# A four-stage attention program on one core: the self-attention values of a decoder kept 64 wide, and a new timetable

## The chip, the cores and the metric

One core of one Trainium2 chip runs the whole program. The time is the device time of one launch in microseconds; lower is better. Everything is fp32.

## The reference, cut to what matters

Four attention stages follow each other on two batches of 512 tokens, 128 wide, with a context of 77 rows, 64 wide. Stages L0, L1 and L3 are short. Stage L2 is a decoder of 6 layers, 16 heads of width 64:

```python
def _mha(s, t, kv_w, q_w, o_w, o_b, mask):
    k, v = jnp.split(s @ kv_w, 2, axis=-1)
    k, v, q = (_heads(k), _heads(v), _heads(t @ q_w))
    scores = jnp.einsum('bhqd,bhkd->bhqk', q, k) * D ** (-0.5)
    scores = jnp.where(mask[:, None] == 0, jnp.float32(-1000000000.0), scores)
    attn = jax.nn.softmax(scores, axis=-1)
    o = jnp.einsum('bhqk,bhkd->bhqd', attn, v)
    return o.transpose(0, 2, 1, 3).reshape(...) @ o_w + o_b

def step(t, p):                                   # one layer, 6 of them
    tn = _ln(t, norm_g, norm_b); t = _mha(tn, tn, skv, sq, sow, sob, tgt_mask) + t
    tn = _ln(t, norm_g, norm_b); t = _mha(src, tn, ckv, cq, cow, cob, src_mask) + t
    tn = _ln(t, pg, pb);         t = t + (jax.nn.relu(tn @ w1 + b1) @ w2 + b2)
```

The mask inputs leave at most the last 128 of the 512 tokens as keys of the self attention (the first 384 or more have a 0 in the mask, and what is 0 is masked out), so the kernel has a path, the unit `FAST`, in which a self-attention head has 128 keys. A flag computed on the chip chooses between it and a general path (`WIDE`), which the inputs here don't take.

## The kernel before, in words

The work of a layer is in four phases: self attention of batch 0 and of batch 1 (s0, s1), cross attention of batch 0 and of batch 1 (x0, x1). A phase is a list of chunks, each 128 query tokens by a group of heads: in self attention 4 groups of 4 heads, 4 chunks each. A group of four heads is two pairs of heads; a pair is 128 of the 1024 head columns.

For each chunk TensorE makes the scores of all heads of the group (`scores`, line 969: one matmul, 512 columns for self attention), VectorE adds the mask by a minimum and takes the row minimum (line 1363), ScalarE takes the exponentials one head at a time (line 1156), VectorE takes reciprocals of the sums (line 1371), GpSimd multiplies (line 642), TensorE transposes the weights block by block (`turn`, line 979), and ScalarE or VectorE copies them to the tile `PT` (lines 1166 and 1380), which has two places, one for each of two groups in flight. When all four chunks of a group are there, TensorE multiplies by the values (`attend`, line 999). All groups of a phase accumulate in one PSUM bank, `sum`. At the end of the phase ScalarE evicts that bank to `oT` (line 1186), TensorE turns it back (`fin`, line 822), VectorE adds it to `X` (line 1283) and normalises (lines 1206 to 1217), and TensorE turns the result (`xn`, line 828).

The output projection of self attention is folded into the values. For each layer and batch two jobs `v` make the values of 512 head columns each, transposed, 128 keys wide (four matmuls of 128 columns, line 775), VectorE copies them to `vT`, and two jobs `V` multiply them head by head with `sa_ow` (line 813: 16 instructions of 64 rows, the two heads of a pair on the two row halves of the array, each into a bank of its own). VectorE copies the two banks of each to `GV` (line 1271). So the value of a head is 128 keys by 128 outputs, and `attend` is four matmuls of 512 columns a group, 16 for a layer and batch. The trace shows every full fp32 matmul as two instructions.

The order of work on each engine is written out by a timetable. Time is cut into ticks: a chunk has two ticks in s0 and x1 and one in s1 and x0. At each tick TensorE does, in this order, the scores due, the `attend` matmuls due, the `early` jobs (`xn`), the transposes of the chunk of the tick, then the `jobs`. ScalarE and VectorE take their part of a job one tick later. All jobs share three PSUM banks (`W`) in turn; a job can start when the one three places before it has been evicted. The tuples on lines 131 to 143 place the jobs: `CV_AT` the cross values, `SELF0_AT` and `SELF1_AT` the operands of self attention, `WEIGHTS_AT` the weights of the next layer, `AFTER_*` what follows a phase (evict, `fin`, three steps of the norm, `xn`), `FEED*` the feed-forward part, and `LAST_AT` stage L3. SyncE loads the weights of the next layer as their tiles come free; `load_o` (the weights `saow`) waits for the last `V` job.

Of the kernel before, what the change touches and what calls it, by code (L numbers as in the profile page):

```python
# [14 lines left out]
P = 128  # L15
# [114 lines left out]
LAG = {"out": 3}  # L130
CV0_AT = (13, 17, 18, 24, 25, 26)
CV_AT = (4, 4, 4, 22, 23, 25)
SELF1_AT = (23, 24, 25, 27, 29, 35)
SELF0_AT = (18, 18, 20, 26, 28, 29)
WEIGHTS0_AT = (5, 6, 8, 8, 9, 9, 11, 11, 13, 13, 15, 15, 16, 16)
WEIGHTS_AT = (24, 23, 31, 32, 33, 33, 35, 35, 37, 37, 40, 40, 42, 42, 45, 44)
AFTER_S0 = (1, 5, 6, 6, 8, 10)
AFTER_S1 = (2, 3, 4, 4, 5, 6)
AFTER_X0 = (0, 2, 3, 4, 5, 7)
AFTER_X1 = (2, 3, 4, 4, 5, 7)  # L140
LAST_AT = (8, 10, 12, 13, 17, 18)
FEED0 = ((8, 8, 9, 9), 10, (13, 14, 15, 15))
FEED1 = ((9, 8, 9, 9), 10, (15, 18, 19, 21))


class Unit:


    def __init__(self, name, wide, layers):
# [77 lines left out]
    def self_operands(self, j, b, at, when):  # L227
        for i in range(2):
            kv, keys, values = when[3 * i:3 * i + 3]
            self.jobs[at + kv] += [("k", j, b, i), ("v", j, b, i)]  # L230
            self.jobs[at + keys] += [("G", j, b, i, 0), ("G", j, b, i, 1)]
            self.jobs[at + values] += [("V", j, b, i, 0), ("V", j, b, i, 1)]

# [20 lines left out]
    def place(self):  # L254
        for b in range(B):
            self.normalise(0, ("xn", 0, b, 0), (b, b, b))
            self.early[1 + 4 * b].append(("xn", 0, b, 0))
        self.self_operands(0, 0, 1, (0, 2, 3, 4, 6, 7))
        for (kind, *i), dt in zip(WEIGHTS[2:], WEIGHTS0_AT, strict=True):
# [54 lines left out]
def by_vector(event):  # L314
    return event[0] in ON_VECTOR

# [8 lines left out]
def build(nc, a, out):  # L325
    with ExitStack() as ctx:
# [33 lines left out]
        G, V = GV[:, 0:8, :], GV[:, 8:16, :].rearrange("p s (t e) -> p s t e", t=TB)  # L360
        full_bias = GV[:, 4:12, :]
        Gc = sb("Gc", [P, 2, B, H * M])
        Vc = sb("Vc", [P, B, NBLK, E])
# [72 lines left out]
        def half(h):  # L436
            return slice(h % 2 * D, h % 2 * D + D)

        block = ctx.enter_context(nc.Block())
# [3 lines left out]
        def _(sp):  # L443
# [122 lines left out]
            with sp.Else():  # L566
                for j in range(L):
# [3 lines left out]
                    if j + 1 < L:  # L571
# [98 lines left out]
        def _(pe):  # L670
# [48 lines left out]
            def work(ring, event, l, unit=None):  # L719
# [44 lines left out]
                elif what in ("k", "v"):  # L764
# [31 lines left out]
                elif what == "V":  # L796
                    b = event[2]
                    pe.wait_ge(sem("saow_in"), 16 * n_in)
                    if unit.wide:
                        p, h = divmod(event[3], 2)  # L800
                        made(ring, [("v", j, b, p)], l, fills)
                        for i in range(TB):
                            last = nc.tensor.matmul(w[:, i * P:(i + 1) * P], vT[half(h), i * P:(i + 1) * P],
                                                    saow[half(h), p, :], start=True, stop=True)
                    else:
                        i = event[3]
                        even = (*event[:-1], 0)
                        fills, halves = [even, event], [bank_of(ring, even), w]
                        made(ring, [("v", j, b, i)], l, fills)
                        for c in range(TB):  # L810
                            p = TB * i + c
                            for h in range(2):
                                last = nc.tensor.matmul(halves[h][:, c * P:(c + 1) * P], vT[half(h), c * P:(c + 1) * P],  # L813
                                                        saow[half(h), p, :], start=True, stop=True)
                                if c == TB - 1 and h == 0:
                                    last.then_inc(sem(ring.full(even)), 1)
                elif what == "fin":
# [131 lines left out]
            def decoder(unit, l):  # L949
# [33 lines left out]
                def attend(g, blk):  # L983
                    group = unit.groups[g]
                    j, b = group.j, group.b
                    k = group.starts[blk + 1] - group.starts[blk]
                    if blk == 0:
# [4 lines left out]
                        if not group.cross:  # L992
                            values = [("V", j, b, group.index // 2, h) for h in range(2)]
                            made(ring, [("V", j, b, group.index)] if unit.wide else values, l)
                        elif group.first:
# [31 lines left out]
        def _(act):  # L1027
# [13 lines left out]
            def work(ring, event, l, unit=None):  # L1041
# [22 lines left out]
                elif what == "xn":  # L1064
# [7 lines left out]
                    last = nc.scalar.activation(XT[:, b * T:(b + 1) * T], w[:], ACT.Identity, bias=bb, scale=g)  # L1072
                elif what == "k3":
                    key_copy("L3", w)
# [72 lines left out]
            def decoder(unit, l):  # L1147
# [12 lines left out]
                def evacuate_turned(n):  # L1160
# [3 lines left out]
                    if gr >= 2 and qt < 2:  # L1164
                        act.wait_ge(sem(f"{unit.name}_attended"), l * len(unit.groups) + gr - 1)
                    nc.scalar.activation(PT[:, gr % 2, 0:group.blocks, qt * P:(qt + 1) * P],  # L1166
# [33 lines left out]
        def _(dve):  # L1200
# [42 lines left out]
            def work(ring, event, l, unit=None):  # L1243
# [19 lines left out]
                elif what == "v":  # L1263
                    last = nc.vector.tensor_copy(vT[:], w[:])
                elif what == "V":
                    b, i = event[2:4]
                    if unit.wide:
                        last = nc.vector.tensor_copy(V[:, 4 + i % 4, :, :], tiles(w[:]))
                    else:
                        dst = V[:, b * TB + 2 * i:b * TB + 2 * i + 2, :, :].rearrange("p s (n h) e -> p h s n e", h=2)  # L1270
                        last = nc.vector.tensor_copy(dst[:, event[4]], w[:].rearrange("p (s n e) -> p s n e", s=2, n=2))
                elif what == "v3":
# [73 lines left out]
            def decoder(unit, l):  # L1346
# [27 lines left out]
                def evacuate_turned(n):  # L1374
# [3 lines left out]
                    if gr >= 2 and qt < 2:  # L1378
                        dve.wait_ge(sem(f"{unit.name}_attended"), l * len(unit.groups) + gr - 1)
                    nc.vector.tensor_copy(PT[:, gr % 2, 0:group.blocks, qt * P:(qt + 1) * P],  # L1380
# [73 lines left out]
```

## Time and profile before

| | |
|---|---|
| median of 3 runs | 1122.32 us (1119.98 to 1122.93) |
| profiled execution, own time | 1118.3 us |
| its span | 1116.5 us |
| TensorE matmul busy | 1037.2 us (93%) |
| ScalarE busy | 776.3 us (70%) |
| VectorE busy | 742.2 us (66%) |
| GpSimd busy | 391.6 us (35%) |

The profile is of one execution. Busy time is a union of the records of an engine, and a matmul's record is longer than the time until the next one can start, so the spacing of starts says more of TensorE than its busy share. "Idle before" is the time an engine waited ahead of an instruction, and the arrow names what ended the wait.

### The profile page before, as it was taken

To read this page: it belongs to the slowest core of one execution; us is meant where nothing else is said; L and a number is where in the kernel's file an instruction comes from. 1 tells how busy PE (TensorE), PEld (TensorE's weight loads), DVE (VectorE), ACT (ScalarE), POOL (GpSimd) and SP (SyncE) were. 2 spreads that over 40 slices of the span, in tenths; PEclk is the share of its full clock that TensorE was granted. 3 is DMA by queue.
4 is the path that set the end of the run, shared out by engine and by line. 5 is a ranking of instruction groups with operands and counts; after the bars stand their busy time and mean duration, and the time that the engine had idled before them with its cause. 6 is when DMAs were issued, how large, how long until landed. Compare 5 with 4: busy or idle time off the path is not lost.

```text
span 1116.5 us, 21037 instructions
## 1 busy us (share of the span) xinstructions
PE 1037.2 (93%) x5379; PEld 654.3 (59%) x5379; DVE 742.2 (66%) x4557; ACT 776.3 (70%) x3460; POOL 391.6 (35%) x404
## 2 busy tenths in 40 slices
PE   7499999899999899999899999899999899999985
PEld 5466555566655666655556655566655566655543
DVE  4466678765578756578756678855677856667844
ACT  3276798666698666599666689656688857589841
POOL 4122343323353223344323344323344323344421
PEclk9999999999999999999999999999999999999997
DMA  7501300002200002200001400000320000000000
GB/s 197 113 1 58 84 1 2 1 1 76 69 17 1 1 1 66 75 20 1 1 1 33 107 21 1 1 1 1 82 78 1 1 2 1 21 1 1 1 1 19
DMA packets 36952, 32.42 MB, mean 29 GB/s; under 512 B 10202, under 2 KB 31834, under 8 KB 36058
## 3 DMA queue, kind: packets, MB, share of 16 engines
q1 hardware_dynamic: 36826, 31.00, 10.5%
q8 instruction: 47, 0.77, 0.3%
q14 instruction: 79, 0.65, 0.2%
HBM read 30.47 MB, written 0.52 MB: 28 GB/s over the span
## 4 chain that ended last, share of the span: by engine, by line
PE 80%; DVE 10%; issue 5%; ACT 2%; SPq 1%; DVEq 1%; POOL 1%; DMA 1%; ACTq 0%; POOLq 0%
PE sum L999 23%; PE S L969 22%; PE T L979 11%; PE W L833 4%; PE W L864 4%; PE W L775 4%; PE W L762 2%; PE W L813 2%; DVE Pb L1363 2%; PE W L792 2%; PE W L828 2%; DVE XN L1217 1%; DVE PT L1380 1%; DVE stats L1206 1%; DVE X L1283 1%
## 5 line engine op out<-in xcount | busy, mean ns | idle before, releaser
L1156 ACT ACTIVATE Pb<-Pb,mn 128x128 f32<-128x128 f32 (+1 forms) x1536 | 560.8, 370 | 82.7 <-DVE mn L1363 82.4
L642 POOL TENSOR_TENSOR Pb<-Pb,rsum 128x512 f32<-128x512 f32 (+2 forms) x336 | 324.2, 968 | 622.4 <-DVE rsum L1371 622.1
L1156 ACT ACTIVATION_READ_ACCUMULATOR Pb<-Pb,mn 128x1 f32 x1536 | 293.0, 191 | 0.0
L1363 DVE CUSTOM_DVE_ANT_0 Pb<-S,late_bias 128x128 f32<-128x128 f32 x768 | 175.5, 286 | 130.3 <-PE S L969 129.8
L979 PEld LDWEIGHTS T<-ident,Pb 128*128 128x128 f32 (+2 forms) x1296 | 165.7, 147 | 154.7 <-issue 125.6
L969 PE MATMUL S<-GV,XT 128*128 128x512 f32 x384 | 198.2, 603 | 1.6 <-DVE mn L1363 0.8
L979 PE MATMUL T<-ident,Pb 128*128 128x128 f32 (+2 forms) x1296 | 197.5, 274 | 0.2 <-POOL Pb L642 0.2
L999 PE MATMUL sum<-PT,GV 128*128 128x512 f32 x384 | 193.2, 595 | 0.0
L1380 DVE COPY PT<-T 128x512 f32<-128x512 f32 (+1 forms) x240 | 157.4, 656 | 47.7 <-PE T L979 46.4
L1363 DVE CUSTOM_DVE_ANT_0 Pb<-S,cross_bias 128x77 f32<-128x77 f32 x768 | 132.7, 233 | 66.1 <-PE S L969 62.5
L999 PE MATMUL sum<-PT,Vc 128*128 128x512 f32 (+2 forms) x264 | 135.6, 603 | 0.0
L969 PE MATMUL S<-Gc,XT 128*128 128x462 f32 (+1 forms) x288 | 126.2, 520 | 6.9 <-DVE mn L1363 6.9
L1363 DVE DVE_READ_ACCUMULATOR2_ANT mn<- 128x1 f32 x1536 | 126.6, 82 | 0.2
L999 PEld LDWEIGHTS sum<-PT,GV 128*128 128x128 f32 x384 | 67.9, 191 | 57.2 <-issue 56.5
L969 PEld LDWEIGHTS S<-GV,XT 128*128 128x128 f32 x384 | 63.1, 190 | 44.9 <-issue 32.0
L1166 ACT ACTIVATE PT<-T 128x512 f32<-128x512 f32 x96 | 56.1, 584 | 23.8 <-PE T L979 23.4
L606 POOL TENSOR_TENSOR rstd<-veps,minus_half 128x4 f32<-128x4 f32 x40 | 40.5, 1011 | 79.1 <-DVE veps L1212 77.4
L999 PEld LDWEIGHTS sum<-PT,Vc 128*128 128x128 f32 (+2 forms) x264 | 46.0, 190 | 32.5 <-issue 26.8
L1371 DVE RECIPROCAL rsum<-sums 128x4 f32<-128x4 f32 (+1 forms) x336 | 58.5, 174 | 0.3
L969 PEld LDWEIGHTS S<-Gc,XT 128*128 128x128 f32 x288 | 45.6, 192 | 21.5 <-issue 13.3
L1217 DVE TENSOR_SCALAR XN<-X,mv,rstd 128x128 f32<-128x128 f32 x152 | 50.2, 390 | 3.4 <-issue 3.4
L828 PE MATMUL W<-ident,XN 128*128 128x128 f32 x144 | 23.1, 285 | 28.7 <-DVE XN L1217 19.1
(159 smaller groups left out, 1042.6 us busy)
## 6 DMA issues: line engine op xcount, KB each, us to landing
sakv<-in_L_xattn_sa_kv SPq DMA_DIRECT2D x6, 1024.0 KB, 5.5
saq<-in_L_xattn_sa_q SPq DMA_DIRECT2D x6, 512.0 KB, 5.9
saow<-in_L_xattn_sa_ow SPq DMA_DIRECT2D x6, 512.0 KB, 3.9
cakv<-in_L_xattn_ca_kv SPq DMA_DIRECT2D x12, 256.0 KB, 7.5
caq<-in_L_xattn_ca_q SPq DMA_DIRECT2D x6, 512.0 KB, 8.5
w<-in_L_xattn_ff_w SPq DMA_DIRECT2D x12, 256.0 KB, 3.1
caow<-in_L_xattn_ca_ow SPq DMA_DIRECT2D x30, 96.0 KB, 4.1
GV<-in_mask_BxSxS_ik SPq DMA_DIRECT2D x1, 2048.0 KB, 9.9
```

Of the source, the lines that this page charges most:

```text
L642: nc.gpsimd.tensor_tensor(rows, rows, r, ALU.mult).then_inc(sem(f"{unit.name}_weights"), 1)
L775: last = nc.tensor.matmul(w[:, p * P:(p + 1) * P], sakv[:, c:c + P], XT[:, b * T + KEYS:(b + 1) * T], start=True, stop=True)
L828: last = nc.tensor.transpose(w[:, t * P:(t + 1) * P], XN[:, b * TB + t, :], ident[:])
L969: nc.tensor.matmul(S_ps[n % 2][:, 0:group.columns], XT[:, (b * TB + qt) * P:(b * TB + qt + 1) * P], keys, start=True, stop=True).then_inc( ...
L979: last = nc.tensor.transpose(T_ps[n % 2][0:k1 - k0, t * P:(t + 1) * P], Pb[:, n % SLOTS, k0:k1], ident[:])
L999: mm = nc.tensor.matmul(sum_ps[:], vals, PT[0:k, g % 2, blk, :], start=(group.first and blk == 0), stop=(group.last and at_end))
L1156: last = nc.scalar.activation(Pb[:, s, t * w:(t + 1) * w], Pb[:, s, t * w:(t + 1) * w], ACT.Exp, bias=mn[:, s, t:t + 1], scale=-1.0, accum ...
L1166: nc.scalar.activation(PT[:, gr % 2, 0:group.blocks, qt * P:(qt + 1) * P], tiles(T_ps[n % 2][:, 0:group.blocks * P]), ACT.Copy)\
L1217: last = nc.vector.tensor_scalar(dst[:, t, :], X[:, t, :], mv[:, t, 0:1], rstd[:, t:t + 1], ALU.subtract, ALU.mult)
L1363: last = nc.vector.tensor_tensor_reduce(out=Pb[:, s, cols], in0=S_ps[n % 2][:, cols], in1=row_bias, scale=1.0, scalar=3.4e38, op0=ALU.add, ...
L1371: nc.vector.reciprocal(rsum[:, n % SLOTS, 0:k], sums[:, n % SLOTS, 0:k])\
L1380: nc.vector.tensor_copy(PT[:, gr % 2, 0:group.blocks, qt * P:(qt + 1) * P], tiles(T_ps[n % 2][:, 0:group.blocks * P]))\
```

## The change

`v` becomes one matmul of 512 columns, with the 128 tokens as the stationary operand; its result, keys by head columns, is copied to `v_own`, which lies where four of the eight value slots of `GV` were. The `V` jobs of the fast path go. New jobs `o` come, one for each pair of heads, the two of a group in the same tick: two matmuls of 512 columns, each with 64 stationary columns (one head's values), one into partitions 0 to 63 and one into partitions 64 to 127 of the same `W` bank. VectorE evicts the even pair and ScalarE the odd one to `o_pair`. Two ticks after that, `attend` multiplies `o_pair` with `saow`: one matmul of 512 columns a pair. A place of `PT` is free when the `o` job of the odd pair is done. `load_o` waits for the end of s1's attention instead of the last `V` job. The timetable gets new numbers. The other edits tell the wide path's `V` from the fast one.

```diff
-CV0_AT = (13, 17, 18, 24, 25, 26)
-CV_AT = (4, 4, 4, 22, 23, 25)
-SELF1_AT = (23, 24, 25, 27, 29, 35)
-SELF0_AT = (18, 18, 20, 26, 28, 29)
-WEIGHTS0_AT = (5, 6, 8, 8, 9, 9, 11, 11, 13, 13, 15, 15, 16, 16)
-WEIGHTS_AT = (24, 23, 31, 32, 33, 33, 35, 35, 37, 37, 40, 40, 42, 42, 45, 44)
-AFTER_S0 = (1, 5, 6, 6, 8, 10)
-AFTER_S1 = (2, 3, 4, 4, 5, 6)
+CV0_AT = (13, 15, 18, 21, 25, 26)
+CV_AT = (4, 5, 7, 22, 26, 28)
+SELF1_AT = (23, 25, 27, 31)
+SELF0_AT = (18, 18, 26, 28)
+WEIGHTS0_AT = (6, 6, 11, 11, 12, 12, 15, 15, 17, 18, 19, 19, 20, 21)
+WEIGHTS_AT = (23, 25, 30, 32, 33, 33, 35, 35, 37, 37, 40, 40, 42, 42, 45, 44)
+AFTER_S0 = (3, 4, 5, 6, 8, 9)
+AFTER_S1 = (2, 3, 4, 7, 8, 9)
 AFTER_X0 = (0, 2, 3, 4, 5, 7)
 AFTER_X1 = (2, 3, 4, 4, 5, 7)
-LAST_AT = (8, 10, 12, 13, 17, 18)
-FEED0 = ((8, 8, 9, 9), 10, (13, 14, 15, 15))
-FEED1 = ((9, 8, 9, 9), 10, (15, 18, 19, 21))
+LAST_AT = (12, 14, 14, 17, 18, 19)
+FEED0 = ((8, 8, 9, 9), 10, (13, 14, 15, 17))
+FEED1 = ((9, 9, 9, 9), 10, (18, 18, 20, 21))
...
+            if not group.cross and not wide:
+                first = self.end[group.j, group.phase % 4] if group.last else self.tick_of[(g + 1) * TB]
+                for i in range(TB // 2):
+                    fill = first + 1
+                    self.jobs[fill].append(("o", group.j, group.b, 2 * group.index + i))
+                    self.attend[fill + 2].append((g, i))
+                continue
...
-                        emptied(FAST, ("V", j, 1, 1, 1), 0)
+                        sp.wait_ge(sem("fast_oT"), 4 * j + 2)
                         load_o(j + 1)
...
+                    elif what == "v":
+                        last = nc.tensor.matmul(w[:], XT[:, b * T + KEYS:(b + 1) * T], sakv[:, c0 + i * T:c0 + (i + 1) * T],
+                                                start=True, stop=True)
...
+                elif what == "o":
+                    b, p = event[2:4]
+                    g = unit.first_group[4 * j + b] + p // 2
+                    made(ring, [("v", j, b, p // TB)], l, fills)
+                    if p % 2 == 0:
+                        for i in range(2):
+                            pe.wait_ge(sem(f"{unit.name}_turned_sb{i}"), (g + 1) * (TB // 2))
+                    for h in range(2):
+                        c = (2 * p + h) % 8 * D
+                        last = nc.tensor.matmul(w[half(h), :], v_own[:, b, p // TB, c:c + D], PT[:, g % 2, p % 2 * 2 + h, :],
+                                                start=True, stop=True)
...
+                    if not group.cross and not unit.wide:
+                        p = 2 * group.index + blk
+                        if group.first and blk == 0:
+                            pe.wait_ge(sem("saow_in"), 16 * (j + 1))
+                            if group.phase > 0:
+                                pe.wait_ge(sem(f"{unit.name}_oT"), group.phase)
+                        made(ring, [("o", j, b, p)], l)
+                        mm = nc.tensor.matmul(sum_ps[:], saow[:, p, :], o_pair[:, p % 2, :], start=(p == 0), stop=(p == NPAIR - 1))
+                        if blk == 1:
+                            mm.then_inc(sem(f"{unit.name}_attended"), 1)
+                        return
```

## Rows read from the trace of the kernel before

**Rows 1.** The page's first part: busy time of each engine, whole execution.
```profile
PE 1037.2 (93%) x5379; PEld 654.3 (59%) x5379; DVE 742.2 (66%) x4557; ACT 776.3 (70%) x3460; POOL 391.6 (35%) x404
```

**Rows 2.** The chain that ended last: shares by engine, then by line.
```profile
PE 80%; DVE 10%; issue 5%; ACT 2%; SPq 1%; DVEq 1%; POOL 1%; DMA 1%; ACTq 0%; POOLq 0%
PE sum L999 23%; PE S L969 22%; PE T L979 11%; PE W L833 4%; PE W L864 4%; PE W L775 4%; PE W L762 2%; PE W L813 2%; DVE Pb L1363 2%; PE W L792 2%; PE W L828 2%; DVE XN L1217 1%; DVE PT L1380 1%; DVE stats L1206 1%; DVE X L1283 1%
```

**Rows 3.** Stretches s0, s1, x0 of layer 2: length, busy by engine, clock, DMA.
```profile
401.80:458.00 56.20, 55.83 (x327) 36.97 (x326) 35.63 (x196) 37.15 (x148) 18.74 (x18) 1.00 0.14 39
458.00:495.30 37.30, 37.30 (x177) 21.82 (x176) 26.34 (x170) 30.14 (x133) 16.43 (x16) 1.00 0.22 63
495.30:522.70 27.40, 25.68 (x109) 15.11 (x109) 21.94 (x166) 24.64 (x133) 12.21 (x14) 1.00 0.01 1
```

**Rows 4.** The chain in order of time, layer 2: start, us, what.
```profile
396.53 1.79 PE W L775 x16
...
404.20 1.09 PE W L813 x16
405.29 1.06 PE sum L999 x2
...
407.53 0.86 PE sum L999 x2
```

**Rows 5.** Groups by form, whole execution: count, busy us, mean ns, idle before.
```profile
L999 PE MATMUL sum<-PT,GV 128*128 128x512 f32 x384 | 193.2, 595 | 0.0
L1166 ACT ACTIVATE PT<-T 128x512 f32<-128x512 f32 x96 | 56.1, 584 | 23.8 <-PE T L979 23.4
L1271 DVE COPY GV<-W 128x512 f32<-128x512 f32 x48 | 30.7, 682 | 7.0 <-PE W L813 7.0
L813 PE MATMUL W<-saow,vT 64*128 64x128 f32 x384 | 27.9, 284 | 2.4 <-DVE Vc L1262 1.0 <-issue 0.7 <-ACT GV L1063 0.7
```

**Rows 6.** Line 813 between 404.1 and 404.3 us: durations, starts.
```profile
L813 PE MATMUL W<-saow,vT x2: 374/374/374, 404.1 to 404.1; 64*128 64x128 f32 x2
```

**Rows 7.** Timeline of TensorE at the turn from s1 to x0, layer 1.
```profile
336.99 0.60 PE L979 MATMUL T<-ident,Pb 128*128 128x128 f32 x4
...
338.64 0.60 PE L822 MATMUL W<-ident,oT 128*128 128x128 f32 x4
...
343.12 0.79 PE L969 MATMUL S<-Gc,XT 128*128 128x308 f32 x2 [1.11 <-DVE mn L1363]
...
345.38 0.63 PE L828 MATMUL W<-ident,XN 128*128 128x128 f32 x4 [0.61 <-DVE XN L1217]
```

**Rows 8.** Timeline of VectorE ahead of that wait.
```profile
341.75 0.38 DVE L1210 BATCH_NORM_AGGREGATE mv<-stats 128x2 f32<-128x6 f32 x4
342.20 0.17 DVE L1212 TENSOR_SCALAR veps<-mv 128x4 f32<-128x4 f32 x1
342.35 0.24 DVE L1363 CUSTOM_DVE_ANT_0 Pb<-S,cross_bias 128x77 f32<-128x77 f32 x1
```

**Rows 9.** Timeline of TensorE, three later waits, x1 of layer 1 and s0 of layer 2.
```profile
363.31 0.63 PE L822 MATMUL W<-ident,oT 128*128 128x128 f32 x4 [0.43 <-ACT oT L1186]
...
393.46 0.63 PE L828 MATMUL W<-ident,XN 128*128 128x128 f32 x4 [0.73 <-DVE XN L1217]
...
421.04 1.16 PE L813 MATMUL W<-saow,vT 64*128 64x128 f32 x16 [0.20 <-DVE Vc L1262]
```

**Rows 10.** Timeline of TensorE at the end of the last layer.
```profile
1077.72 0.60 PE L673 MATMUL W<-ident,X 128*128 128x128 f32 x4
...
1079.02 1.07 PE L853 MATMUL W<-XT,L0G 128*77 128x512 f32 x2
1079.92 2.74 PE L999 MATMUL sum<-PT,Vc 128*128 128x512 f32 x6
...
1088.95 1.09 PE L828 MATMUL W<-ident,XN 128*128 128x128 f32 x4 [4.79 <-DVE XN L1217]
```

**Rows 11.** DMA issues: size, us to landing.
```profile
saow<-in_L_xattn_sa_ow SPq DMA_DIRECT2D x6, 512.0 KB, 3.9
```

More of the change, by code:

```diff
@@ L228, in self_operands @@
         for i in range(2):
-            kv, keys, values = when[3 * i:3 * i + 3]
+            kv, keys = when[2 * i:2 * i + 2]
             self.jobs[at + kv] += [("k", j, b, i), ("v", j, b, i)]
             self.jobs[at + keys] += [("G", j, b, i, 0), ("G", j, b, i, 1)]
-            self.jobs[at + values] += [("V", j, b, i, 0), ("V", j, b, i, 1)]
     def last_attention(self, b, at, steps):
@@ L257, in place @@
             self.early[1 + 4 * b].append(("xn", 0, b, 0))
-        self.self_operands(0, 0, 1, (0, 2, 3, 4, 6, 7))
+        self.self_operands(0, 0, 1, (0, 2, 4, 6))
         for (kind, *i), dt in zip(WEIGHTS[2:], WEIGHTS0_AT, strict=True):
@@ L314, in by_vector @@
 def by_vector(event):
-    return event[0] in ON_VECTOR
+    return event[0] in ON_VECTOR or event[0] == "o" and event[3] % 2 == 0
 def turned_by_vector(unit, n):
@@ L361, in build @@
         full_bias = GV[:, 4:12, :]
+        v_own = GV[:, 8:12, :].rearrange("p (b i) n -> p b i n", b=B)
+        o_pair = sb("o_pair", [P, 2, T])
         Gc = sb("Gc", [P, 2, B, H * M])
@@ L437, in half, with transposed_read @@
             return slice(h % 2 * D, h % 2 * D + D)
+        def transposed_read(unit, g, l):
+            group = unit.groups[g]
+            if group.cross or unit.wide:
+                return f"{unit.name}_attended", l * len(unit.groups) + g + 1
+            pair = ("o", group.j, group.b, 2 * group.index + 1)
+            return unit.ring.full(pair), unit.ring.value(pair, l)
         block = ctx.enter_context(nc.Block())
@@ L798, in work @@
                     pe.wait_ge(sem("saow_in"), 16 * n_in)
[L799 to L816, printed above, removed]
+                    p, h = divmod(event[3], 2)
+                    made(ring, [("v", j, b, p)], l, fills)
+                    for i in range(TB):
+                        last = nc.tensor.matmul(w[:, i * P:(i + 1) * P], vT[half(h), i * P:(i + 1) * P],
+                                                saow[half(h), p, :], start=True, stop=True)
+                elif what == "o":
[9 more added lines that the diff above has]
+                                                start=True, stop=True)
                 elif what == "fin":
@@ L992, in attend @@
                         if not group.cross:
-                            values = [("V", j, b, group.index // 2, h) for h in range(2)]
-                            made(ring, [("V", j, b, group.index)] if unit.wide else values, l)
+                            made(ring, [("V", j, b, group.index)], l)
                         elif group.first:
@@ L1072, in work @@
                     last = nc.scalar.activation(XT[:, b * T:(b + 1) * T], w[:], ACT.Identity, bias=bb, scale=g)
+                elif what == "o":
+                    last = nc.scalar.activation(o_pair[:, event[3] % 2, :], w[:], ACT.Copy)
                 elif what == "k3":
@@ L1164, in evacuate_turned @@
                     if gr >= 2 and qt < 2:
-                        act.wait_ge(sem(f"{unit.name}_attended"), l * len(unit.groups) + gr - 1)
+                        name, value = transposed_read(unit, gr - 2, l)
+                        act.wait_ge(sem(name), value)
                     nc.scalar.activation(PT[:, gr % 2, 0:group.blocks, qt * P:(qt + 1) * P],
@@ L1263, in work @@
                 elif what == "v":
-                    last = nc.vector.tensor_copy(vT[:], w[:])
+                    last = nc.vector.tensor_copy(vT[:] if unit.wide else v_own[:, event[2], event[3], :], w[:])
+                elif what == "o":
+                    last = nc.vector.tensor_copy(o_pair[:, event[3] % 2, :], w[:])
                 elif what == "V":
[L1266 to L1271, printed above, removed]
+                    last = nc.vector.tensor_copy(V[:, 4 + event[3] % 4, :, :], tiles(w[:]))
                 elif what == "v3":
@@ L1378, in evacuate_turned @@
                     if gr >= 2 and qt < 2:
-                        dve.wait_ge(sem(f"{unit.name}_attended"), l * len(unit.groups) + gr - 1)
+                        name, value = transposed_read(unit, gr - 2, l)
+                        dve.wait_ge(sem(name), value)
                     nc.vector.tensor_copy(PT[:, gr % 2, 0:group.blocks, qt * P:(qt + 1) * P],
```

## The prediction

> **What bounds the kernel now.** I read the busy shares first: TensorE is busy 93% of the span and no other engine over 70% [rows 1]. The chain that ended last agrees: 80% of it is TensorE, and its two largest lines are the attention product, line 999, and the scores, line 969 [rows 2]. Then the stretches by phase: in s0 and s1 TensorE is busy all the time while ScalarE has 19 and 7 us of slack; in x0 the two are within 1 us of each other, 25.68 and 24.64 of 27.40 us [rows 3]. So a matmul saved in self attention is time saved, and ScalarE has to be watched from the end of s1 on. Last the timeline of TensorE, which shows a few waits that repeat in every layer: on VectorE's row minimum and on the norm at the turn to x0 [rows 7], on a norm in x1 and on a copy of cross values in s0 [rows 9].
>
> **The stream of TensorE, part by part, for one layer and batch (12 of them).** A 512-column fp32 matmul on the whole array takes 0.86 us on the chain [rows 4].
>
> Before: two `v` jobs (with two `k` jobs, 16 instructions in 1.79 us, so 0.90 each [rows 4]) take 1.79. A `V` job takes 1.09, and the matmul behind it 1.06 in place of 0.86 [rows 4], so 1.29, and two take 2.58. The 16 matmuls of `attend` take 13.76. (384 records of two to a matmul are 192, that is 16 for each of the 12 [rows 5].) Sum 18.13 us.
>
> After: two `v` matmuls 1.72; 8 `attend` matmuls with `saow` 6.88; and 16 `o` matmuls of 64 stationary columns. These are the open price; the trace before has no matmul on half the columns. Both ends: each takes the array's full time, 16 x 0.86 = 13.76, or two heads run side by side, 8 x 0.86 = 6.88. The nearest row is the `V` job, where two heads lie on two row halves: its first two instructions start at the same 404.1 us [rows 6], and its 16 instructions of 128 columns are through in 1.09, where 16 such on the whole array, those of `k` and `v`, take 1.79 [rows 4]. I take the side-by-side value. Going into and out of the half-array form costs something: of the 1.29 us of a `V` job 0.86 is its stream (8 pairs of instructions of a quarter of 0.43 each), so 0.43 is the price of one switch in and out. The two pairs of a group are together, so there are 4 such switches, 1.72 us. (Some of the 0.43 could hide under a matmul four times as long; at 0.2 it would be 0.8.) Sum after: 1.72 + 6.88 + 6.88 + 1.72 = 17.20. That is 0.93 less, **11.2 us less over 12**; with the cheaper switch 22 us less; with no overlap 24.08, so 71 us more.
>
> A rule of the Trainium skill speaks against the side-by-side value. "TensorE: Matmul & The Clock Gate", section "The mechanism" of its part on packing small matmuls, says that a weight load overlaps a running matmul only when its row group differs; the two column halves have the same rows. By the strict reading the second head's matmul could not start beside the first, and the result is the first rival below. The trace does not bear out the strict reading for the whole array: a load on all rows never adds to the 0.86 us spacing [rows 4]. The same page's section "Measured speedup vs the span model" gives 2.38 times for three column tiles, which is for overlap, though not perfect. No row here shows column halves.
>
> **Evictions.** VectorE loses 4 copies of 682 ns (`V`) [rows 5] and gets 4 of about the same size (`o`, even pairs): nothing. ScalarE gets 4 new ones; at the 584 ns of its copy of the same shape [rows 5] that is 2.3 us in each of s0 and s1, which brings it to 39.5 of 56.2 and 32.5 of 37.3 us [rows 3]. Hidden by TensorE as long as each is done within a tick: `attend` comes two ticks after `o`. Behind that wait on TensorE stand the transposes and scores of the next chunk. I take 3 us in all for late ones (48 groups; 0 if never, 0.58 each or 28 us if each comes one copy late).
>
> **The turns of the phases.** The norm after s1 has its second and third step at ticks 7 and 8 instead of 4 and 5. The aggregate and the addition of epsilon stand straight before the row minima for which TensorE waits, 341.75 to 342.35, 0.60 us [rows 8]; without them the 1.11 us wait should lose 0.6: 6 layers, -3.6. The `xn` after it comes three ticks later, so its 0.61 wait [rows 7] goes: -3.7. The `xn` of the next layer comes two ticks later (`FEED0`), its 0.73 [rows 9] goes, 5 times: -3.6. The 0.20 wait ahead of a `V` job [rows 9] goes, 5 times: -1.0. Against it: the last `attend` of s1 now is in the tick of `fin`. Before, the transposes (336.99) and another chunk stood between it and `fin` (338.64) [rows 7], so no wait; now it is as at the end of x0, where `fin` waits 0.43 for the eviction [rows 9]: 6 times, +2.6. ScalarE waits a tick longer for that last `attend` at the end of s1, and a tick less at the end of s0 (eviction due at tick 3 instead of 1, product in tick 3): I let these cancel, though x0 is where ScalarE has no slack [rows 3]; a tick there is 27.4/12 = 2.3 us, so 0 to 2.3 a layer, up to 14 us if none of it is absorbed.
>
> **The end.** Stage L3's scores of batch 0 leave the dense part for the gap in which TensorE waits 4.79 us for the norm [rows 10]. The transposes and the score matmul there take 0.44 and 0.90 (1079.02 to 1079.92) [rows 10]: -1.3.
>
> **The load of `saow`** starts at the turn to x0 instead of in s1, lands in 3.9 us [rows 11], and is first needed in the next s0, more than a cross phase later. On SyncE nothing stands behind it that waits for less than the end of the layer. I take nothing for it, and see no way in which it could gain.
>
> **Sum.** -11.2 - 3.6 - 3.7 - 3.6 - 1.0 - 1.3 + 2.6 + 3.0 = -18.8 us. From the profiled execution's own time, 1118.3 (span 1116.5 and 1.8 around it), that is 1099.5. The runs shown have a median 4.0 us higher; taken from it, 1122.3 - 18.8 = **1103.5 us**.
>
> **Rivals.**
> 1. The column halves don't overlap. +71 for the stream in place of -11.2, the turns as above: 1122.3 + 71 - 7.6 = 1186. For it: no row shows halves of columns, and the rule above. Against it: the row halves' common start [rows 6]. This is the slower side, and it decides as soon as a pair of `o` matmuls takes more than about 1.06 us instead of 0.86 (there are 96 pairs, and 18.8 over 96 is 0.2).
> 2. They overlap with a stagger: a matmul is two instructions of 0.43, and if the second head starts only behind the first head's second one, each group costs one more 0.43, 48 x 0.43 = 20.6: 1124. Against it: both records at 404.1 [rows 6].
> 3. ScalarE becomes late. Eviction of the odd pair behind a batch of exponentials holds `attend`, and the wait at the end of s1 isn't absorbed in x0: up to 28 + 14; half of it, 18 more than my 3, gives 1122. For it: 24.64 of 27.40 in x0; against it: 7 us of slack in s1 [rows 3].
> 4. Only the stream gains, and other waits take the place of those at the turns (the same chains of VectorE, GpSimd and ScalarE run later): without the -11.9 of the turns 1115.
> 5. The stream gains more: cheap switches, 22 instead of 11.2: 1093.
>
> **How the numbers follow.** Forecast with its neighbourhood (1096 to 1110) 45%, case 5 (below 1096) 12%, case 4 16%, cases 2 and 3 together 13%, no overlap 14%. The range for 8 in 10 runs from 1090 to 1125: it leaves out no overlap and the ends. A measurement of this kernel can tell about 0.3%, 3.4 us, from no change. Faster by more: 45 + 12 + 16 and 4 of the 13, 77%. Within: 5 of the 13. Slower: 14 + 4, 18%.
>
> **What would show it.** Line of `o`: records in pairs with the same start, two pairs in about 2.1 us from first start to the next whole-array matmul. About 13.8 and not 27.5 us of TensorE for them in a layer. Wrong if the starts are 0.43 or 0.86 apart. The waits before the `xn` transposes at both places gone, `fin` at the end of s1 waiting some 0.4 us for `oT`, s0 and s1 together 2 us shorter in a layer, x0 1 us shorter. If ScalarE is late, TensorE's `attend` on `o_pair` waits for ScalarE's copy, and x0 is longer than 27.4 us.

## The result, and the profile after

The changed kernel takes 1115.8 us (median of 6 runs, 1113.6 to 1117.2) against 1122.6 for the kernel before (6 runs, 1119.9 to 1127.2). The ratio is 0.9937, 95% interval 0.9912 to 0.9962: 7 us faster, where 18.8 were forecast. The profiled execution took 1116.8 us, its span is 1114.9.

The page of the changed kernel: busy time, then the chain by engine and by line. To be read against [rows 1, 2].

```profile
PE 1032.8 (93%) x5043; PEld 606.3 (54%) x5043; DVE 736.2 (66%) x4557; ACT 801.5 (72%) x3508; POOL 391.6 (35%) x404
...
PE 81%; DVE 9%; issue 4%; ACT 3%; SPq 1%; POOL 1%; DMA 1%; DVEq 0%; ACTq 0%; POOLq 0%
PE S L986 22%; PE T L996 11%; PE sum L1026 10%; PE W L832 8%; PE sum L1010 7%; PE W L850 4%; PE W L881 4%; PE W L778 3%; PE W L811 2%; PE W L794 2%; DVE Pb L1390 2%; DVE XN L1247 2%; PE W L789 2%; PE W L845 2%; PE W L769 1%
```

TensorE is still the bound. `o` (line 832) has 8% of the chain and the new `attend` (line 1010) 7%; the old `attend` on `GV` and the `V` jobs are gone. ScalarE has 25 us more, VectorE 6 us less.

Line 832 of the changed kernel, between 467.5 and 467.7 us, and the timeline of TensorE around that group:

```profile
L832 PEld LDWEIGHTS W<-PT,GV x4: 132/134/136, 467.5 to 467.6; 128*64 128x64 f32 x4
L832 PE MATMUL W<-PT,GV x2: 643/643/643, 467.5 to 467.6; 128*64 128x512 f32 x2
```
```profile
467.02 0.60 PE L996 MATMUL T<-ident,Pb 128*128 128x128 f32 x4
467.55 1.94 PE L832 MATMUL W<-PT,GV 128*64 128x512 f32 x8
469.42 1.12 PE L986 MATMUL S<-GV,XT 128*128 128x512 f32 x2
470.38 0.60 PE L996 MATMUL T<-ident,Pb 128*128 128x128 f32 x4
```

The two column halves run side by side: two records begin within a tenth of a microsecond, and the 8 instructions of the two pairs of a group, 3.44 us one after the other, are through in 1.87. From the start of the transposes to the start of the next ones 3.36 us pass; the transposes take 0.44, the scores 0.86, the eight instructions two by two 4 x 0.43 = 1.72. The rest, 0.34, is one switch into and out of the column halves, where I took 0.43.

Stretches of layer 2, each from the first transposes of a phase to those of the next: s0 and s1 of the kernel before, then s0, s1, x0, x1 of the changed one. (Those of [rows 3] start 7 to 10 us earlier, at the scores. Cut at the transposes, ScalarE has 4.5 us of slack in s1 of the kernel before, not 7, and 2 us in the changed one.)

```profile
409.10:468.00 58.90, 58.70 (x351) 39.71 (x350) 35.38 (x195) 38.89 (x151) 19.71 (x20) 1.00 0.21 59
468.00:504.30 36.30, 36.30 (x154) 20.33 (x153) 27.18 (x194) 31.78 (x152) 18.21 (x18) 1.00 0.10 29
```

```profile
407.40:465.70 58.30, 57.24 (x313) 35.25 (x312) 35.28 (x194) 39.79 (x153) 20.23 (x20) 1.00 0.19 56
465.70:502.10 36.40, 36.40 (x154) 18.30 (x153) 26.90 (x187) 34.33 (x155) 17.82 (x18) 1.00 0.08 20
502.10:529.50 27.40, 26.31 (x113) 14.72 (x112) 23.16 (x176) 24.64 (x132) 10.85 (x13) 1.00 0.07 20
529.50:578.70 49.20, 44.71 (x241) 28.01 (x240) 32.15 (x185) 31.65 (x141) 13.55 (x16) 0.97 0.00 1
```

I summed TensorE's starts in these stretches, taking 0.43 us for an instruction of 512 columns. "Stream" is that sum, with a side-by-side pair once, "small" what spacings have more than it up to 0.15 us (the switches are in it), "waits" what is over 0.15:

| layer 2, us, before / after | length | stream | small | waits |
|---|---|---|---|---|
| s0 | 58.9 / 58.3 | 55.5 / 53.8 | 2.6 / 2.6 | 0.4 / 1.6 |
| s1 | 36.2 / 36.3 | 35.4 / 34.6 | 0.8 / 1.7 | 0 / 0 |
| x0 | 27.3 / 27.5 | 24.9 / 24.9 | 0.4 / 0.9 | 2.1 / 1.8 |
| x1 | 49.2 / 49.2 | 39.2 / 38.3 | 3.8 / 3.6 | 5.8 / 6.8 |

The stream lost 3.4 us a layer and the switches gave 1.1 back: -2.3, or 13.9 over 6 layers, more than the 11.2 forecast. But the "waits" grew by 1.9. Of the 6.8 us in x1 about 1.2 are no waits: they are spacings of instructions at half clock, as shown below. In s0 there are three spacings over 0.15 us (0.40 for GpSimd, 0.96 for the norm, and 0.19 ahead of line 811, for which the trace names no cause) where there was one, for which the trace gives a wait of 0.20 [rows 9]; in x1 the wait for `XN` ahead of `k` became a wait for `XT` behind it. The other layers differ a little: in layers 1 to 5 these spacings of s0 come to 1.1 to 1.6 us, against 0.4 before, and in layer 0 to 4.0 against 2.0. TensorE's timeline, the instructions that waited:

```profile
395.93 1.13 PE L794 MATMUL W<-XT,sakv 128*128 128x128 f32 x8 [0.64 <-ACT XT L1099]
```
```profile
437.91 0.66 PE L996 MATMUL T<-ident,Pb 128*128 128x128 f32 x4 [0.24 <-POOL Pb L658]
...
445.74 0.52 PE L845 MATMUL W<-ident,XN 128*128 128x128 f32 x3 [0.80 <-DVE XN L1247]
```
```profile
510.51 0.63 PE L839 MATMUL W<-ident,oT 128*128 128x128 f32 x4 [0.43 <-ACT oT L1216]
...
523.87 0.66 PE L986 MATMUL S<-Gc,XT 128*128 128x462 f32 x1 [0.35 <-DVE mn L1390]
```

And x1, which lost a `V` job, is not shorter. Its granted clock says why. Four microseconds in the middle of x1, of the kernel before (layers 1 and 2) and of the changed one (layers 2 and 3); the third number from the end is the granted clock:

```profile
372.50:376.50 4.00, 4.00 (x18) 2.56 (x16) 3.90 (x22) 2.16 (x12) 0.96 (x1) 0.59 0.01 2
545.60:549.60 4.00, 4.00 (x23) 2.27 (x20) 3.90 (x20) 3.20 (x14) 0.96 (x1) 1.00 0.02 4
```
```profile
543.50:547.50 4.00, 4.00 (x20) 2.83 (x19) 3.69 (x19) 2.16 (x12) 0.96 (x1) 0.64 0.00 0
714.60:718.60 4.00, 4.00 (x19) 3.02 (x18) 3.69 (x19) 2.17 (x12) 0.96 (x1) 0.50 0.01 2
```

Before, two of the first five layers had a stretch at half clock (1.2 GHz) there, and their x1 is 50.6 us long; the other three were at 2.4 GHz throughout and have 48.9 to 49.2. Changed, all five have it: 49.1 to 49.2, and 50.6 in layer 3, where it lasts longest. Of the changed kernel, layer 2, the two waits that it comes behind:

```profile
538.67 0.60 PE L996 MATMUL T<-ident,Pb 128*128 128x128 f32 x4
540.57 0.63 PE L845 MATMUL W<-ident,XN 128*128 128x128 f32 x4 [1.30 <-DVE XN L1247]
543.15 1.91 PE L757 MATMUL W<-ctxT,cakv 64*128 64x154 f32 x12 [1.96 <-issue]
545.00 1.40 PE L986 MATMUL S<-Gc,XT 128*128 128x308 f32 x2
```

The second wait is put down to "issue", but the job needs the bank that VectorE is still emptying into `vTb`: that copy ends at 543.06, and the job starts at 543.15. The kernel before has both waits too, 1.1 and 2.0 us in layers 1 and 2 alike, and its clock fell behind them in layer 1 and not in layer 2. So the two waits alone do not decide it.

### The profile page after: what moved, and what is told of

It reads as the page before. It is cut to its first block, busy times and chain, and to the rows that moved or that the text cites. A ratio compares the mean times of both kernels' runs of the same rounds, so it can differ in the third digit from the quotient of the medians.

```text
span 1114.9 us, 20402 instructions
## 1 busy us (share of the span) xinstructions
PE 1032.8 (93%) x5043; PEld 606.3 (54%) x5043; DVE 736.2 (66%) x4557; ACT 801.5 (72%) x3508; POOL 391.6 (35%) x404
## 4 chain that ended last, share of the span: by engine, by line
PE 81%; DVE 9%; issue 4%; ACT 3%; SPq 1%; POOL 1%; DMA 1%; DVEq 0%; ACTq 0%; POOLq 0%
PE S L986 22%; PE T L996 11%; PE sum L1026 10%; PE W L832 8%; PE sum L1010 7%; PE W L850 4%; PE W L881 4%; PE W L778 3%; PE W L811 2%; PE W L794 2%; DVE Pb L1390 2%; DVE XN L1247 2%; PE W L789 2%; PE W L845 2%; PE W L769 1%
## 5 line engine op out<-in xcount | busy, mean ns | idle before, releaser
L986 PE MATMUL S<-Gc,XT 128*128 128x462 f32 (+1 forms) x288 | 128.7, 533 | 3.4 <-DVE mn L1390 2.1
L832 PE MATMUL W<-PT,GV 128*64 128x512 f32 x384 | 93.2, 605 | 0.3 <-ACT wqTc L1076 0.3
L1010 PE MATMUL sum<-o_pair,saow 128*128 128x512 f32 x192 | 90.2, 592 | 0.0
L1196 ACT ACTIVATE PT<-T 128x512 f32<-128x512 f32 x96 | 56.3, 587 | 26.0 <-PE T L996 24.9
L1398 DVE RECIPROCAL rsum<-sums 128x4 f32<-128x4 f32 (+1 forms) x336 | 58.3, 174 | 2.3 <-ACT Pb L1185 1.9
L1010 PEld LDWEIGHTS sum<-o_pair,saow 128*128 128x128 f32 x192 | 35.5, 190 | 39.2 <-issue 38.7
L1113 ACT ACTIVATE hT<-W,small 128x512 f32<-128x512 f32 x48 | 32.9, 687 | 31.9 <-PE W L850 31.9
```

Source lines behind the costliest of these rows:

```text
L832: last = nc.tensor.matmul(w[half(h), :], v_own[:, b, p // TB, c:c + D], PT[:, g % 2, p % 2 * 2 + h, :], start=True, stop=True)
L986: nc.tensor.matmul(S_ps[n % 2][:, 0:group.columns], XT[:, (b * TB + qt) * P:(b * TB + qt + 1) * P], keys, start=True, stop=True).then_inc( ...
L1010: mm = nc.tensor.matmul(sum_ps[:], saow[:, p, :], o_pair[:, p % 2, :], start=(p == 0), stop=(p == NPAIR - 1))
L1398: nc.vector.reciprocal(rsum[:, n % SLOTS, 0:k], sums[:, n % SLOTS, 0:k])\
```

## The experiments

All ratios are to the kernel before on the same chip, 95% intervals in brackets. The changed kernel is at 0.9937.

### Halves of the change: e_mech and e_table

```diff
 # e_mech, the changed kernel with the old places
+SELF1_AT = (23, 24, 27, 29)
+AFTER_S0 = (3, 5, 6, 6, 8, 10)
 # ... all other tuples of lines 131 to 143 as before
```


> The changed kernel's jobs with the old timetable (only the eviction at the end of s0 stays at tick 3, since the products end there). Theory A: the 64-wide values are worth their stream, 3.4 us a layer less, less 1.1 us of switches, 14 us in all, and the new timetable adds nothing or takes some away: 1106 to 1112 us. Theory B: the new places carry the gain and the new jobs in the old places run into waits: 1118 or more.

```diff
 # e_table, the kernel before with the new places
+SELF1_AT = (23, 25, 26, 27, 31, 35)
 # SELF0_AT as before, all other tuples as changed
```


> The kernel before with the new timetable, its V jobs left at their old distances (that of the first pair half in s0 one tick later). Theory A (the table moves waits from one norm to another and gains nothing, as the traces of before and after show 8.2 and 10.1 us of waits over 0.15 us in layer 2): 1120 to 1127 us. Theory B (the table is what gained): 1112 to 1117. The prediction's terms for the turns, 11.9 less and 2.6 more, would give 1113.

e_mech: 1118.0 us, 0.9965 [0.9948, 0.9983]. e_table: 1127.5 us, 1.0053 [1.0037, 1.0070]. The old kernel is 6 us slower with the new places, so theory B is out for the table alone, and so is the prediction's pricing of the turns (1113). The clock has a part in the 6 us: in e_table's trace x1 is at half clock in all five layers, in that of the kernel before in two. But at the same mean granted clock it is still 4 to 5 us slower (at 0.987, 1125.9 us against 1120.6 to 1122.1), so most of it is the places. The new jobs in the old places bring only 4 us, not the 10 to 16 of theory A either. Something took the gain of both. In e_mech's trace x1 is at half clock for 3 to 7 us in four of five layers (49.4 to 50.5 us) and at full clock in layer 0, where it takes 47.6; and its s0 has a new wait, too (below). The wait of 0.24 for GpSimd is there as in the changed kernel, and once more in s1, so it is not the new places' doing:

```profile
422.61 0.63 PE L845 MATMUL W<-ident,XN 128*128 128x128 f32 x4 [0.48 <-DVE XN L1247]
```

### The price of the halves and of a switch: e_full and e_split

```diff
 # e_full
-    c = (2 * p + h) % 8 * D
-    ... matmul(w[half(h), :], v_own[:, b, p // TB, c:c + D], ...
+    c = 2 * p % 8 * D
+    ... matmul(w[:], v_own[:, b, p // TB, c:c + P], ...
 # e_split
-    fill = first + 1
+    fill = first + 1 + (0 if group.last else i)
```


> The changed kernel with both heads of a pair on the whole array, one after the other: each o matmul takes the 128 columns of the pair and writes all 128 partitions, so the output is not the reference's; it measures the time without column halves and without switches. If the stream of TensorE is on the path: 96 pairs x 0.86 more, 48 switches x 0.34 less, 66 us more than the changed kernel, 1182 us. If ScalarE or VectorE set the pace in self attention, less: below 1165.

> The changed kernel with the two pairs of a group in two ticks, one tick apart, except for the last group of a phase: 36 more switches into and out of the column halves. If a switch costs the 0.34 us that the trace of the changed kernel shows and stands on the path: 12 us more, 1128. If it costs the 0.43 of the prediction 1131. If it is hidden: 1116.

e_full: 1180.5 us, 1.0534 [1.0513, 1.0554], 65 us over the changed kernel where 66 were worked out. Its group of line 832, by form, against 93.2 us busy for the same 384 instructions in the changed kernel:

```profile
L832 PE MATMUL W<-PT,GV 128*128 128x512 f32 x384 | 172.7, 592 | 0.0
```

So TensorE's stream in self attention is on the path one for one, and rival 1 (1186) is about what would have been without side-by-side halves. e_split: 1123.0 us, 1.0012 [0.9992, 1.0032], 8 us over the changed kernel; 36 switches at 0.34 would be 12. In its trace s1 is 1.1 us longer, 3 switches at 0.34, and in s0 about 0.2, so there they partly fall into waits. Putting both pairs of a group into one tick is worth having. Two single pairs in s1:

```profile
477.64 1.08 PE L832 MATMUL W<-PT,GV 128*64 128x512 f32 x4
478.65 1.12 PE L986 MATMUL S<-GV,XT 128*128 128x512 f32 x2
480.15 1.08 PE L832 MATMUL W<-PT,GV 128*64 128x512 f32 x4
```

### The clock: e_fill, b_fill and e_mech_fill

```diff
                 elif what == "xn":
                     made(ring, [], l, fills)
+                    if unit is FAST and event[3] == 2 and b == 0:
+                        for _ in range(6):
+                            nc.tensor.matmul(w[:, 0:P], ident[:], ident[:], start=True, stop=True)
 ...
                     fills, halves = [keys, event], [bank_of(ring, keys), w]
+                    if unit is FAST and j > 0 and i == 1:
+                        made(ring, [], l, [keys])
+                        for _ in range(8):
+                            nc.tensor.matmul(halves[0][:, 0:P], ident[:], ident[:], start=True, stop=True)
                     made(ring, [], l, fills)
```


> The changed kernel with work that nobody uses on TensorE in the two waits of x1 after tick 6: 6 small matmuls of the identity by itself ahead of the wait for the norm (1.3 us), 8 ahead of the wait for the copies of the cross values (1.7 us). Theory A (what x1 gains by losing a V job is eaten by TensorE's clock, granted at half for 3 to 4 us behind these waits in every layer): the clock stays full in x1 in most layers, x1 goes from 49.2 to 47.6 us, the whole 5 to 9 us faster than the changed kernel, 1107 to 1111 us, although work is added. Theory B (the clock is a bystander): x1 as long as before or longer, 1116 to 1120.

> The kernel before with the same unused matmuls in the same two waits of x1. Its trace had half clock in x1 in 2 of 5 layers, at 1.4 us each. Theory A (the clock took more from the changed kernel than from the old one): 2 to 5 us less than the kernel before, 1117 to 1120, so that with the clock held full the change is worth 10 to 13 us and not 7. Rival (the unused matmuls gain the same 8 to 9 us on the old kernel, and the clock has nothing to do with the change): 1113 to 1115.

> The changed kernel's jobs in the old timetable, with the unused matmuls in x1 so that the clock stays full there. The old kernel with them took 1116.7, the changed one 1106.7. Theory A (the new jobs are worth their stream less the switches, 2.3 us a layer, and the table gains nothing on top): 1103 to 1107. Theory B (the table carries part of the gain): 1109 to 1113.

e_fill: 1106.7 us, 0.9861 [0.9840, 0.9882]. Three microseconds of unused matmuls in a layer make the kernel 9 us faster. Its x1 is 47.4 to 47.7 us in all five layers, at full clock. The same place in its trace, timeline and four microseconds:

```profile
536.91 0.60 PE L1003 MATMUL T<-ident,Pb 128*128 128x128 f32 x4
537.58 1.60 PE L849 MATMUL W<-ident 128*128 128x128 f32 x12
539.02 0.60 PE L852 MATMUL W<-ident,XN 128*128 128x128 f32 x4
539.46 1.95 PE L755 MATMUL W<-ident 128*128 128x128 f32 x16
541.39 1.06 PE L761 MATMUL W<-ctxT,cakv 64*128 64x154 f32 x12
542.38 0.79 PE L993 MATMUL S<-Gc,XT 128*128 128x308 f32 x2
```
```profile
541.80:545.80 4.00, 4.00 (x22) 2.24 (x19) 3.90 (x22) 3.23 (x14) 0.96 (x1) 1.00 0.00 0
```

From the transposes to the cross job pass 4.48 us, as in the changed kernel (538.67 to 543.15): the waits are as long as they were, only filled. What is gained is behind them: 12 instructions of line 757 had taken 1.85 us to the next start, and take 0.99.

b_fill: 1116.7 us, 0.9939 [0.9921, 0.9956]: the kernel before gains 6 to 7 us from it, less than the changed one but more than I expected. The profiled run of the kernel before had the half clock in two layers, which is 2.8 us, but that is its fastest run (1118.3 us). The others, run beside the experiments, fall into two groups, and in each, but for one run, the time goes with the mean granted clock: from 1119.1 us at 0.990 to 1128 at 0.982, and from 1119.7 at 0.973 to 1127 and more at 0.963. (I take the second group to have the half clock in the first 60 us as well, as the profile of the changed kernel has, from 17 to 58 us. That costs nothing: layer 0's first transposes start at 69.0 us there, and at 69.6 in the profile of the kernel before, which is at full clock.) So the other 4 us are most likely the clock too, in more layers than its profile shows; there is no trace of such a run to show where. The time lies between the two theories: filling these waits gives 9 us to the changed kernel and 7 to the old one.

e_mech_fill: 1107.5 us, 0.9866 [0.9841, 0.9891]. With the clock held full in x1 the new jobs alone are worth 8 us (0.9866 against 0.9939), and the new places on top nothing that can be measured (0.9861). Phase by phase, b_fill against e_fill, layers 1 to 4: s0 58.9 and 58.0 to 58.3 us, s1 36.2 and 36.3, x0 27.3 and 27.5, x1 48.9 to 49.2 and 47.4 to 47.7. Most of what is gained lies in x1, just where the clock hid it. In the traces the mean of layers 1 to 4 is 171.5 us for b_fill, 170.1 for e_mech_fill, 169.5 for e_fill; what e_fill gains there, 0.6 a layer, it gives back at the end, where its last x1 is 70.7 us and not 69.3.

### The other waits: e_feed1, e_cv1, e_x1, e_fin, e_xn16

```diff
 # e_feed1
-FEED1 = ((9, 9, 9, 9), 10, (18, 18, 20, 21))
+FEED1 = ((9, 9, 9, 9), 10, (15, 18, 19, 21))
 # e_cv1: WEIGHTS_AT 35, 35, 37, 37 -> 36, 36, 38, 38
 # e_x1: as e_cv1, AFTER_X0 = (0, 2, 3, 4, 5, 8), FEED0 = ((9, 9, 10, 10), 11, (14, 15, 16, 17))
 # e_fin: AFTER_S1 = (2, 4, 5, 7, 8, 9)
 # e_xn16: FEED0 = ((8, 8, 9, 9), 10, (13, 14, 15, 16))
```


> The changed kernel with the norm steps of batch 1's next layer back at 15, 18, 19 (xn at 21 as before), where the new table has 18, 18, 20. Theory A (the new wait of 0.7 to 1.0 us for this norm in s0 comes of its last step standing one tick ahead of xn): the wait goes, five times, 1111 to 1113 us. Rival (VectorE's earlier steps now hold the row minima, and the wait comes back there): 1116 or more.

1108.5 us, 0.9878 [0.9859, 0.9897], more than theory A said. s0 is 57.2 to 57.3 us in layers 1 to 5 instead of 58.0 to 58.3, and `xn` has no wait:

```profile
444.02 0.60 PE L996 MATMUL T<-ident,Pb 128*128 128x128 f32 x4
444.46 0.60 PE L845 MATMUL W<-ident,XN 128*128 128x128 f32 x4
```

That is 4.3 of the 6.6 us. The rest in the profiled run is one x1 at full clock (47.5) and an end 2.2 us shorter; whether the edit causes either I can't say.

> The changed kernel with the second and third cross-key and cross-value jobs one tick later (36, 36, 38, 38 in place of 35, 35, 37, 37), so that TensorE does the scores and transposes of the next chunk while VectorE copies the first ones. Theory A (the waits of x1 are real and the clock falls behind them): the 2.1 us wait shrinks to under 1, five times, and the half clock is rarer: 1103 to 1110 us. Rival (the wait only moves to the hidden layer behind it): 1114 to 1117.

1112.0 us, 0.9908 [0.9888, 0.9929], between the two theories. The clock is full in x1 in all five layers (48.4 to 48.5 us), but the wait is only partly gone, and a new one stands behind it, ahead of the hidden layer, as the rival has it:

```profile
541.74 1.06 PE L757 MATMUL W<-ctxT,cakv 64*128 64x154 f32 x12 [0.88 <-issue]
...
545.30 1.10 PE L850 MATMUL W<-XT,w 128*128 128x512 f32 x2 [1.45 <-DVE kTc L1282]
```

> As the run with later cross jobs, and also xn after the cross attention of batch 0 at tick 8 instead of 7, with the feed-forward jobs of batch 0 one tick later. Theory A: both waits of x1, 1.4 and 2.1 us, are gone or under 0.5 and the clock stays full, 8 to 15 us: 1101 to 1108. Rival (the feed-forward chain is now late for the k and v jobs of the next layer): no faster than the run with the later cross jobs alone.

1124.3 us, 1.0017 [1.0003, 1.0030]: theory A is out and the rival's "no faster" holds, but it is 12 us slower than e_cv1, which neither had. Five waits in x1 where there were two, none long, and the clock at half again in four layers. Of the 12 us, 5 are in the last x1 (74.4 us against 69.4), where 22 us instead of 15 are at half clock. Layer 2:

```profile
543.41 0.63 PE L845 MATMUL W<-ident,XN 128*128 128x128 f32 x4 [0.78 <-DVE XN L1247]
544.46 0.66 PE L996 MATMUL T<-ident,Pb 128*128 128x128 f32 x4 [0.42 <-POOL Pb L658]
546.00 1.06 PE L757 MATMUL W<-ctxT,cakv 64*128 64x154 f32 x12 [0.88 <-issue]
547.67 1.98 PE L1026 MATMUL sum<-PT,Vc 128*128 128x512 f32 x2 [0.62 <-issue]
549.97 2.54 PE L850 MATMUL W<-XT,w 128*128 128x512 f32 x4 [0.32 <-ACT XT L1099]
```

> The changed kernel with fin at tick 4 instead of 3 after s1, and the first norm step a tick later. The prediction's term for fin behind the last product, 0.43 us in each of 6 layers (the trace of the changed kernel shows just that wait): 2.6 us less, 1113. Rival (the norm behind it is now late for its own xn, whose wait of 0.3 us grows): 1115 to 1118.

1121.7 us, 0.9974 [0.9956, 0.9992], 4 us slower than the changed kernel and slower than either theory had it. `fin` waits no more, and the wait of `xn`, which the rival had growing, is as before (0.31 between starts). But TensorE now waits for VectorE's row minima and its copy to `PT`, and x0 is 28.1 us instead of 27.5. I take it that the addition and the norm, a tick later, stand ahead of them; that is not shown:

```profile
518.36 0.79 PE L986 MATMUL S<-Gc,XT 128*128 128x308 f32 x2 [0.35 <-DVE mn L1390]
...
522.50 1.10 PE L1026 MATMUL sum<-PT,Vc 128*128 128x512 f32 x2 [0.43 <-DVE PT L1408]
```

> The changed kernel with the xn of batch 0's next layer at tick 16 instead of 17. The old table had it at 15 and waited 0.9 to 1.2 us for the norm; the new one at 17 makes the k job behind it wait 0.75 us for ScalarE. If both are the same late norm: at 16 neither is waited for in full, 0.5 to 0.7 us a layer, 1112 to 1114. Rival (what is saved at xn is waited for at the scores, 0.48 us there now): 1115 to 1117.

1117.5 us, 0.9944 [0.9925, 0.9963], the same as the changed kernel. At 16 the whole wait for the norm is back, so the norm is what is late, and its place on TensorE decides nothing:

```profile
568.06 0.63 PE L845 MATMUL W<-ident,XN 128*128 128x128 f32 x4 [1.02 <-DVE XN L1247]
```

### A version that beats both: e_best, and b_fill_end beside it

```diff
 # e_best: e_fill and e_feed1, and ahead of xn of batch 1 in the last layer 16 unused matmuls
+                    if unit is FAST and event[3] == 2 and (b == 0 or j == L - 1):
+                        for _ in range(6 if b == 0 else 16):
 # b_fill_end: the same filling on the kernel before
```


> The changed kernel with the unused matmuls in x1, the norm steps of batch 1 back at 15, 18, 19, and 16 unused matmuls more ahead of the last layer's wait for the norm of batch 1 (3.9 us), where the clock is at half during the feed-forward matmuls behind it (8 instructions in 6.0 us instead of 3.4). If the three add up: 1106.7 less 4 to 5 for the norm steps and 2 to 3 for the end, 1099 to 1101. If the norm steps gained only through the clock: 1104 to 1106.

> The kernel before with the unused matmuls in x1 and ahead of the last wait for the norm, and nothing else changed. If the end gains as much as in the best version, 2 to 3 us: 1114 us. The best version, 1100.6, would then be 13 us ahead of it at the same clock.

e_best: 1100.6 us (1100.4 to 1102.4), 0.9801 [0.9773, 0.9829]. b_fill_end: 1114.5 us, 0.9927 [0.9904, 0.9950]. The expectation took the two to be at the same clock, and they are not quite: in b_fill_end's trace x1 is at full clock in all five layers, but x0 is at half for 3 us in two of them and takes 29.0 us instead of 27.3. In the changed kernel the feed-forward matmuls of the last layer ran at half clock behind a wait of 3.93 us:

```profile
1087.72 5.98 PE L850 MATMUL W<-XT,w 128*128 128x512 f32 x8
```

In e_best the wait is filled and they take 3.6:

```profile
1069.83 3.29 PE L849 MATMUL W<-ident 128*128 128x128 f32 x28
1073.39 0.66 PE L852 MATMUL W<-ident,XN 128*128 128x128 f32 x4 [0.27 <-DVE XN L1254]
...
1075.87 3.60 PE L857 MATMUL W<-XT,w 128*128 128x512 f32 x8
```

## Why the prediction was wrong, point by point

The direction and the mechanism of the stream were right, the size was not, and the time lies inside the range but far from the forecast: 6.8 us gained, not 18.8. What failed is the pricing of the waits. The prediction counted those that the new places take away and none that the new jobs and places make, and it had no term for the clock. By its own steps, over the whole run:

- **Stream and switches**, -11.2: the traces give -13.9, with a switch of 0.34 instead of 0.43. The strict reading of the Trainium skill's sentence on weight loads ("TensorE: Matmul & The Clock Gate", "The mechanism") is not what this chip does: halves on the same rows start together. In the rows of line 832 above four weight loads and two matmuls begin within 0.1 us.
- **Evictions on ScalarE**, +3: `attend` on `o_pair` has no wait over 0.15 us in layer 2; nothing.
- **Row minima at x0**, -3.6: the wait of 1.27 us between starts became two of 0.32 and 0.52: -2.6. **`xn` after s1**, -3.7: 0.78 became 0.31: -2.8. **`fin`**, +2.6: 0.60 between starts, +3.6.
- **`xn` of the next layer**, -3.6: this step failed. The wait of 0.9 to 1.2 us between starts did not go, it became one of 0.75 to 0.8 for `XT` at the `k` job behind it: -1.1. e_xn16 shows that it is one late norm, wherever `xn` stands.
- **Waits that are new, above all in s0**: put at nothing, except 1.0 for the one that was to go. This is the step that failed most. The new `FEED1` put the last norm step one tick ahead of its `xn`, and that and a wait for GpSimd are most of the 1.1 to 1.6 us in layers 1 to 5, against 0.4 before, +4.6; layer 0 has 4.0 us against 2.0. Together +6.6, net of the one wait that goes. e_feed1 takes 0.7 to 1.1 a layer of it back with two numbers. Not all of it is the places: e_mech, with the old ones, has 1.0 us of such waits in s0 of layer 2, 3.7 in layer 0 and 0.4 more in s1. And e_table, with the new places alone, makes the old kernel 6 us slower, some 4 to 5 of them at the same clock.
- **The end**, -1.3: with filled x1 the last x1 is 1.4 longer in e_fill than in e_mech_fill, which has the old places (70.7 against 69.3), with 3 us more of it at half clock; against b_fill (69.7) it is 1.0.
- **The clock**, not in the forecast at all: filling the waits of x1 gives 9 us to the changed kernel and 7 to the old one. That is +2 in the difference. It also hid the gain of x1 in the profile, 1.5 us a layer.

-13.9 - 2.6 - 2.8 + 3.6 - 1.1 + 6.6 + 1.4 + 2 = -6.8; measured -6.8. That it comes out to the tenth is luck: most terms are from one trace, smaller changes in x1 that nearly cancel (`fin` there, the cross jobs) are left out, and without the clock's +2 the sum is -8.8 where b_fill and e_fill differ by 10.0. So of the 12 us that the forecast had too much, some 2 are the clock and some 10 waits.

Of the signs that the prediction named, the records in pairs and the 0.43 us of `fin` for `oT` came. The others did not: one wait of `xn` is left at 0.31 and the other moved, s0 and s1 together are 0.5 us shorter in layer 2 and not 2, and x0 is 0.2 longer and not 1 shorter. Of the rivals, 4 (only the stream gains, other waits take the place of those at the turns; 1115) describes it, at 16%. Open: whether the new places help the new jobs when x1 is not filled (0.9937 against 0.9965, but the intervals overlap) and why then not when it is.

## What to carry to other kernels

Two matmuls with 64 stationary columns each, into the two partition halves of one bank, run side by side in fp32; put several pairs together, since each switch into and out of this form costs a third of a microsecond. When a timetable is changed, price the waits that each new place, and each new job, can make, not only those that it removes: a late norm is waited for somewhere else. When a stage does not get shorter though its work did, look at the granted clock behind its waits, and try unused matmuls in them.

## What the runs showed of the hardware that was not expected

- **The clock and short waits.** Two waits of about 1.3 and 2.0 us with 0.6 us of transposes between them, in a stretch with others of 0.3, are followed by 3 to 7 us at half clock in all five layers of the changed kernel; with the same two filled, in none of 25 layers (e_fill, e_mech_fill, e_best, b_fill, b_fill_end). The kernel before has waits of 1.1 and 2.0 us there, and its profile has the half clock behind them in two layers of five. It comes behind shorter ones, too: in b_fill_end in x0 of two layers, behind waits of 1.11 and 0.61 us.
- **VectorE beside GpSimd.** Three tensor-scalar instructions of the norm (128x128, two scalars each) take 0.85 us when GpSimd is idle and 1.58 where it multiplies. It is one of the three that takes longer: it starts 0.1 us behind the multiplication, lasts 1.07 us and ends 0.08 us after it; the other two take 0.33 each, as ever. Changed kernel, VectorE and GpSimd, and kernel before:

```profile
444.01 1.58 DVE L1247 TENSOR_SCALAR XN<-X,mv,rstd 128x128 f32<-128x128 f32 x3
```
```profile
443.91 1.09 POOL L658 TENSOR_TENSOR Pb<-Pb,rsum 128x512 f32<-128x512 f32 x1 [0.84 <-DVE rsum L1398]
```
```profile
368.50 0.85 DVE L1217 TENSOR_SCALAR XN<-X,mv,rstd 128x128 f32<-128x128 f32 x3
```

The 0.73 us are most of the 0.80 for which `xn` waited in s0.
